# Attention and expert block on one core: the last queries' product and rotation moved among the scores, and transposed scores begun behind 38 scores

## The reference

```
h = layernorm(x)
q, k, v = h @ Wq.T, h @ Wk.T, h @ Wv.T
q, k = rotate(q), rotate(k)                    # q*cos + rotate_half(q)*sin
kf, qf = elu(k) + 1, elu(q) + 1                # linear attention
mem_out = (qf @ (kf.T @ v)) / (qf @ kf.sum)
attn = softmax(q @ k.T / 4) @ v                # per head, over 1024 keys
x = x + (sigmoid(gate)*mem_out + (1-sigmoid(gate))*attn) @ Wo.T
h = layernorm(x); top 2 of 8 experts per token, softmax of their logits
x = x + sum of weighted silu(h @ gate.T) * (h @ up.T) @ down.T
```

## Time and profile before

| | us |
|---|---|
| three runs | 425.9, 426.46, 426.72 |
| median | 426.46 |
| profiled execution | 425.57 |
| its span | 423.4 |

### The profile page before, as it was taken

The page is one execution under the profiler, slowest core; times in us unless marked ns, Lnnn a source line. Parts: engine busy times, 40 slices in busy tenths (PEclk is TensorE's granted clock), DMA queues, the critical chain, the costliest instruction groups (busy, mean ns, idle before and its releaser), DMA issues.

```text
span 423.4 us, 6988 instructions
## 1 busy us (share of the span) xinstructions
PE 398.1 (94%) x2410; PEld 228.3 (54%) x2411; DVE 253.0 (60%) x509; ACT 207.2 (49%) x395; POOL 126.3 (30%) x124
## 2 busy tenths in 40 slices
PE   8998989989999999999999799999999999999982
PEld 3463652223222322432422123699989998997981
DVE  6889889878888797679889601287224232231310
ACT  4429927676676777657566598621112212121110
POOL 6327883040301103011035240204722122312312
PEclk9999999999999999999999999999999999999997
DMA  7236914557350806203013169621544122321342
GB/s 236 106 105 100 302 36 87 95 139 244 90 185 9 263 0 211 72 8 127 2 49 138 50 210 379 181 75 39 167 106 64 25 39 31 46 39 26 37 113 25
DMA packets 22876, 45.05 MB, mean 106 GB/s; under 512 B 4448, under 2 KB 15584, under 8 KB 22016
## 3 DMA queue, kind: packets, MB, share of 16 engines
q0 software_dynamic: 9216, 30.28, 25.3%
q1 hardware_dynamic: 13152, 14.00, 12.9%
q10 hardware_dynamic: 480, 0.39, 0.3%
HBM read 23.76 MB, written 15.59 MB: 93 GB/s over the span
## 4 chain that ended last, share of the span: by engine, by line
PE 65%; DVE 11%; DMA 6%; SPq 5%; ACT 4%; issue 3%; POOL 3%; ACTq 1%; DVEq 0%; POOLq 0%
PE psum L1378 62%; DVE mem L1082 5%; DMA mem<-mem 3%; SPq L471 2%; POOL xg_d L705 2%; DMA mem<-x 2%; SPq L468 1%; DMA mem<-xg_d 1%; ACT mem L898 1%; SPq L498 1%; PE psum L1519 1%; PE psum L1651 1%; DVE mem L1025 1%; DMA xg_d<-mem 1%; ACT mem L811 1%
## 5 line engine op out<-in xcount | busy, mean ns | idle before, releaser
L1378 PE MATMUL psum<-mem 128*32 128x512 f32 (+15 forms) x2278 | 387.1, 401 | 14.7 <-DVE mem L1082 3.9
L1378 PEld LDWEIGHTS psum<-mem 128*128 128x128 f32 (+8 forms) x2278 | 215.0, 144 | 174.3 <-issue 67.1
L1082 DVE TENSOR_REDUCE mem<-psum 128x1 f32<-128x1024 f32 x128 | 152.2, 1217 | 30.4 <-PE psum L1378 28.6
L898 ACT ACTIVATE mem<-psum 128x512 f32<-128x512 f32 x256 | 137.5, 605 | 62.1 <-PE psum L1378 59.2
L916 ACT ACTIVATE mem<-psum 128x384 f32<-128x384 f32 (+3 forms) x32 | 15.1, 471 | 74.8 <-PE psum L1378 68.6
L729 POOL DMA_INDIRECT sum_d<-mem x17 | 26.7, 1570 | 69.8 <-ACT mem L924 41.2
L687 POOL DMA_DIRECT2D mem<-gate_up x21 | 15.2, 729 | 106.9 <-DMA mem<-mem 106.9
L1247 DVE COPY mem<-mem 128x3 f32<-128x3 f32 x18 | 3.0, 167 | 58.9 <-PE psum L1651 54.8
L1260 DVE TENSOR_TENSOR mem<-mem,psum 128x384 f32<-128x384 f32 (+3 forms) x32 | 16.8, 526 | 28.7 <-ACT mem L919 26.7
L924 ACT ACTIVATE mem<-psum,mem 128x256 f32<-128x256 f32 x18 | 8.5, 473 | 39.6 <-PE psum L1378 39.6
L705 POOL DMA_INDIRECT xg_d<-mem x16 | 15.8, 984 | 7.2 <-issue 4.5
(11 more groups left out here) (129 smaller groups left out, 189.3 us busy)
## 6 DMA issues: line engine op xcount, KB each, us to landing
xg_d<-mem POOLq DMA_DIRECT2D x8, 1036.0 KB, 9.5
mem<-gate_up POOLq DMA_DIRECT2D x8, 688.0 KB, 4.4
mem<-gate_up POOLq DMA_DIRECT2D x8, 624.0 KB, 6.6
mem<-down POOLq DMA_DIRECT2D x4, 1024.0 KB, 9.3
mem<-mem SPq DMA_DIRECT2D x54, 64.0 KB, 2.7
mem<-mem SPq DMA_DIRECT2D x18, 128.0 KB, 4.5
mem<-xg_d SPq DMA_DIRECT2D x16, 129.5 KB, 2.4
mem<-x SPq DMA_DIRECT2D x4, 256.0 KB, 4.7
```

Source lines behind the costliest of these rows:

```text
L898: nc.scalar.activation(prob[:, t % 8], psum[:, score_bank(n, t)], ACT.Exp, scale=HD ** -0.5).then_inc(exp_ready, 1)
L1082: V.tensor_reduce(mx[:, par, k:k + 1], banks(2 * (k % 2), 2), AX.X, ALU.max).then_inc(max_ready, 1)
L1378: return nc.tensor.matmul(*a, **k)
```

## The change

The last queries' product leaves the projections. Its four matmuls stand behind scores 1, 3, 5 and 7, in the banks that v had (4 and 5) after two of v's copies. ScalarE copies the raw product to SBUF (`q_raw`), and GpSimd does the whole rotation (`last_queries`: two products of 1024 columns, a difference and a sum of 512). VectorE no longer touches that piece. Scores are issued twice only from 8 to 15, where the transposes now stand (9, 11, 13, 15). The state is made in single products behind each of the scores 16 to 31. Masking the state stands behind the first unit's maxima instead of in front of reduction 14. Linear products 0 and 1 stand behind score 35, 2 and 3 behind 37, 4 and 5 in the loop at steps 1 and 3.

The loop begins behind FIRST = 38 scores; its steps 0 to 5 carry two scores each, until the lead of 44 is reached. ScalarE issues two of the four transfers of unit 0's maxima, and GpSimd the two transfers of first queries' second parts that ScalarE issued. SyncE sends the maxima of unit 1 ahead of `stacks(3)`. GpSimd's fills 0 to 2 no longer stand in the lead but behind `load_gate_up(0)`; the others follow one place later (`FILLS`). The last queries' middle part is made by ScalarE at step 7, and copies 2 to 5 of linear products behind exponentials 0 to 3.

```
-        QK_BANK = [4, 6, 0, 2]
+        QK_BANK = [4, 6, 0, 4]
+        TURN_BANK, STATE_BANK = [6, 7, 4, 5], 6
-        TURN_STEP, STATE_STEP, LIN_STEP = [13, 14, 15, 16], [19, 21, 23, 25], [30, 32, 35, 37, 39, 41]
+        LAST_QUERY, TURN_STEP, STATE_STEP = [1, 3, 5, 7], [9, 11, 13, 15], list(range(16, 32))
+        LIN_STEP, LIN_LATE = [35, 35, 37, 37], {1: 4, 3: 5}
...
             stacks(1)
-            max_rows(0, 0)
+            max_rows(0, 0, range(2))
             sp.wait_ge(lo_ready[1], 3)
             stacks(2)
+            max_rows(1, 1)
+            sp.wait_ge(lo_ready[2], 1)
             stacks(3)
-            sp.wait_ge(lo_ready[2], 1)
-            max_rows(1, 1)
...
+            def last_queries():
+
+                pool.wait_ge(rope_0, 3)
+                pool.wait_ge(q_copied, 2)
+                for k in range(2):
+                    nc.gpsimd.tensor_tensor(tmp[:, 2 * k:2 * k + 2], q_raw,
+                                            rope[:, k, cols(1)].unsqueeze(1).to_broadcast([P, HB, HALF]),
+                                            ALU.mult).then_inc(rope_3, 1)
+                pool.wait_ge(rope_3, 2)
+                nc.gpsimd.tensor_tensor(qT[:, 0, cols(1)], tmp[:, 0], tmp[:, 3], ALU.subtract).then_inc(rope_0, 1)
+                nc.gpsimd.tensor_tensor(qT[:, 1, cols(1)], tmp[:, 1], tmp[:, 2], ALU.add).then_inc(rope_1, 1)
...
             pool.wait_ge(mid_ready[0], 1)
             other(0)
+            pool.wait_ge(mid_ready[0], 2)
+            for g in range(GROUPS):
+                if QPART[g] == 1:
+                    to, part = second_part_rows(1, g)
+                    pool.dma_start(to, part).then_inc(q0_in, 16)
             pool.wait_ge(lo_ready[0], 3)
-            for i in range(1, 4):
+            for i in range(1, 3):
                 other(i)
...
-            FILLS = [(3, 4), (5,), (6,), (7,)]
+            FILLS = [(0, 1, 2), (3, 4), (5, 6), (7,)]
+            pool.wait_ge(xg_set, 1)
...
+            act.wait_ge(qk_ps, 4)
+            for b in range(HB):
+                nc.scalar.copy(q_raw[:, b], psum[:, QK_BANK[3] + b]).then_inc(q_copied, 1)
+            for i in range(2):
+                turned_features(i)
...
+            other_mid(0)
+            act.wait_ge(mT_ready, 1)
+            for b in range(2, 4):
+                act.dma_start(max_row(0, b), mT[32 * b:32 * b + 32]).then_inc(mrow_in, 16)
+            for i in range(1, 3):
+                other_mid(i)
+            for j in range(2):
+                lin_copy(j)
...
+                if isinstance(n, int) and n < 4:
+                    lin_copy(n + 2)
+                if isinstance(n, int) and n == 7:
+                    act.wait_ge(res_ready[2], 1)
+                    mid_part(3, slice(0, HB), resid_3).then_inc(mid_ready[2], 1)
...
-            turns(2, 1).then_inc(rope_mul, 1)
-            first_turn(3)
-            rotated(3, 0).then_inc(rope_0, 1)
-            turns(3, 1).then_inc(rope_mul, 1)
+            turn(2, 1, 1).then_inc(rope_mul, 1)
...
-                if s == 27:
+                if s == STEPS - 1:
                     mask_state()
...
-            for s in range(LEAD):
-                if s in (0, 2):
-                    pe.wait_ge(rope_mul, 3 + s // 2)
-
-                score(0, s, again=s not in TURN_STEP + STATE_STEP + LIN_STEP)
-
+            pe.wait_ge(q0_in, 16 * QPART.count(1))
+            pe.wait_ge(rope_mul, 3)
+            for s in range(FIRST):
+
+                score(0, s, again=s in range(8, 16))
+
+                if s in LAST_QUERY:
+                    k = LAST_QUERY.index(s)
+                    if k == 0:
+                        pe.wait_ge(v_ready, 2)
+                    ins = key_query(3, k // HB, k % HB)
+                    if k == len(LAST_QUERY) - 1:
+                        ins.then_inc(qk_ps, 1)
...
-                if not (isinstance(n, int) and n + LEAD >= ALL):
+                if isinstance(n, int) and n < LEAD - FIRST:
+                    for k in range(2):
+                        score(i, FIRST + 2 * t + k)
+                elif not (isinstance(n, int) and n + LEAD >= ALL):
                     score(i, t + LEAD)
+                if isinstance(n, int) and n in LIN_LATE:
+                    lin_out(LIN_LATE[n])
```

More of the change, by code:

```diff
@@ L436, in place, with queries_in, max_row, second_part_rows @@
             return 2 * i + t // STEPS, t % STEPS, 2 * STEPS * i + t
+        def queries_in(n):
+            return 16 * (GROUPS * n - QPART.count(1))
+        def max_row(sl, b):
+            return qst[SROWS:SROWS + 2, sl].rearrange("p j (k b q) -> p (j k) b q", b=4, q=32)[:, :, b]
+        def second_part_rows(i, g):
+            w, hf = QK_IDX[i]
+            to = slice(g * HD, (g + 1) * HD)
+            return (qst[to, 0] if w else kst[to, 0, :, cols(hf)]), parts[0:4 * HD, w, 1, 0, cols(hf)]
         def gate_up_pieces(to, src):
@@ L628, in _, with rest @@
+            def rest(i):
+                w, hf = QK_IDX[i]
+                pool.wait_ge(hi_ready[1], i + 1)
+                nc.gpsimd.tensor_tensor(resid_1[:, i], (kT, qT)[w][:, 1, cols(hf)], parts[:, w, 0, 1, cols(hf)],
+                                        ALU.subtract).then_inc(res_ready[1], 1)
             pool.wait_ge(mid_ready[0], 1)
             other(0)
+            pool.wait_ge(mid_ready[0], 2)
[3 more added lines that the diff above has]
+                    pool.dma_start(to, part).then_inc(q0_in, 16)
@@ L630, in _ @@
             pool.wait_ge(lo_ready[0], 3)
-            for i in range(1, 4):
+            for i in range(1, 3):
                 other(i)
             for hf in range(2):
-                feature(kfeat, kT, exp_k, hf, hf + 1)
-            pool.wait_ge(xg_set, 1)
-            pool.wait_ge(k0_in, 2 * 16 * GROUPS)
-            pool.wait_ge(q_in, 16 * GROUPS)
-            for e in range(3):
-                fill(e * T, (e + 1) * T)
-            for i in range(3):
-                w, hf = QK_IDX[i]
-                pool.wait_ge(hi_ready[1], i + 1)
-                nc.gpsimd.tensor_tensor(RESID_1[i], (kT, qT)[w][:, 1, cols(hf)], parts[:, w, 0, 1, cols(hf)],
-                                        ALU.subtract).then_inc(res_ready[1], 1)
@@ L645, in _ @@
-            for hf in range(2):
-                feature(qfeat, qT, exp_q, hf, hf + 3)
+                feature(kfeat, exp_k[:, hf], hf, hf + 1)
+            last_queries()
+            feature(qfeat, exp_q[:, :, cols(0)], 0, 3)
+            rest(0)
+            feature(qfeat, exp_q[:, :, cols(1)], 1, 4)
+            for i in range(1, 3):
+                rest(i)
             for i in range(3):
@@ L649, in _ @@
                 pool.wait_ge(mid_ready[1], i + 1)
[L650 removed]
+                nc.gpsimd.tensor_tensor(parts[:, w, 2, 1, cols(hf)], resid_1[:, i], parts[:, w, 1, 1, cols(hf)],
                                         ALU.subtract).then_inc(lo_ready[1], 1)
@@ L876, in _ @@
                                psum[:, LIN_BANK[j], 0:m * LW].rearrange("p (g c) -> p g c", g=m)).then_inc(lin_ready, 1)
+            first_hi(0)
+            first_mid(0)
+            second_keys(0)
+            act.wait_ge(rope_1, 1)
+            negated(exp_k[:, 0], kT, 0)
+            first_hi(1)
+            first_mid(1)
+            positive(kfeat, kT, 0)
+            first_hi(2)
+            grown(exp_k[:, 0], 1)
+            first_mid(2)
+            second_keys(2)
+            for j in range(4):
+                v_copy(j)
+            act.wait_ge(rope_1, 3)
+            negated(exp_k[:, 1], kT, 1)
+            positive(kfeat, kT, 1)
+            grown(exp_k[:, 1], 2)
+            act.wait_ge(qk_ps, 4)
[3 more added lines that the diff above has]
+                turned_features(i)
+            negated(exp_q[:, :, cols(0)], qT, 0)
+            positive(qfeat, qT, 0)
+            grown(exp_q[:, :, cols(0)], 3)
+            for i in range(2, 4):
+                turned_features(i)
+            for i in range(3):
+                hi_part(i, 1).then_inc(hi_ready[1], 1)
+            act.wait_ge(rope_0, 4)
+            act.wait_ge(rope_1, 4)
+            negated(exp_q[:, :, cols(1)], qT, 1)
+            positive(qfeat, qT, 1)
+            grown(exp_q[:, :, cols(1)], 4)
+            hi_part(3, slice(0, HB)).then_inc(hi_ready[2], 1)
+            other_mid(0)
+            act.wait_ge(mT_ready, 1)
+            for b in range(2, 4):
+                act.dma_start(max_row(0, b), mT[32 * b:32 * b + 32]).then_inc(mrow_in, 16)
+            for i in range(1, 3):
+                other_mid(i)
+            for j in range(2):
+                lin_copy(j)
             def turned_copy(hf, n):
@@ L1022, in turn @@
                 m, p = (tmp, tmp_odd)[i % 2], QK_BANK[i]
-                if i >= 2 and not k:
-                    dve.wait_ge((rope_0, rope_1)[b], i - 1)
+                if i == 2 and not k:
+                    dve.wait_ge((rope_0, rope_1)[b], 1)
                 return V.tensor_tensor(m[:, 2 * b + k], psum[:, p + (1 - b if k else b)],
```

120 lines of the change are left out of this document (54 added, 66 removed).

## The result

| | before | changed |
|---|---|---|
| median of 4 runs, us | 426.43 | 432.37 |
| lowest to highest, us | 425.9 to 426.72 | 432.0 to 434.04 |
| profiled execution, us | 425.57 | 432.17 |
| its span, us | 423.4 | 430.2 |
| TensorE's mean granted clock | 0.995 | 0.979 |

Changed over before is 1.0148, 95% interval 1.0116 to 1.0179: the changed kernel is **slower**, by 6 us, and outside the range of the prediction.

What follows compares the result with a forecast made beforehand. Bounds: unit 0's maxima, unit 1's start and SyncE's queue. 1.6 + 1.4 + 0.86 - 0.3 - 2.2 = 1.4 us gained: 424.2 us profiled, 425.1 us forecast median (chance 0.43); range 422.2 to 428.2 us.

Steps and rivals of the forecast that it cites:

- Start of the lead: From the projections to the first reduction: it starts at 32.6 us instead of 34.19 us, 1.6 us gained.
- The lead to the maxima: First to sixteenth reduction of unit 0: 20.4 us instead of 21.8 us, 1.4 us gained; maxima ready at about 54.4 us.
- The four steps behind a sixteenth reduction stay: Between unit 0's sixteenth reduction and its ready maxima: length unchanged, before the change from 56.04 to 57.48 us.
- GpSimd and ScalarE: Beside the lead: last query feature near 52 us, low parts near 58.5 us, second quad's stack about 1.8 us earlier.
- First transposed scores: After unit 0's maxima: no gain, and 0.3 us lost to ScalarE's middle part between two exponentials.
- Gate of unit 1: At step 32: unit 1's maxima land at 81.9 us, needed at 84.9 us; the 0.9 us wait goes, 0.86 us gained.
- What is late next: The fourth quad at step 52: last queries land at 103.3 us, TensorE waits 2.2 us; bounds nothing to 5.1 us.
- 2.1 us a key transfer: Time assumed for each 128 KB key transfer of the fourth quad beside weights and fills, between 1.8 and 3.6 us.
- rival 3: Clock falls to 1.2 GHz in the lead or behind the pause at step 52; 428.5 us or more; chance 0.06.
- Rival 2: Key stack crawls beside the fills, so score 96 waits at a price of 5.1 us; 428.0 us; chance 0.17.
- Behind step 52 the kernels have the same work: After step 52: same work and order except the fills, and a TensorE pause there is not recovered; no size given.
- The mask's wait in the lead: At scores 32 to 38 TensorE waits for the mask, idle about 45% of the time; no term in the sum.

Runs made afterwards that it cites:

- e6: e5 with GpSimd's three low parts of the second halves held until the first maxima are transposed; 424.03 us, ratio 0.9963 to the kernel before.
- e7: The changed kernel with 20 matmuls of ones ahead of its waits for queries at steps 52 and 116; 435.75 us, ratio 1.0196 to the kernel before.
- e1: The changed kernel with SyncE again sending the fourth quad's stack ahead of unit 1's maxima; 430.19 us, ratio 1.0068 to the kernel before.
- e3: The changed kernel with the fourth quad's keys issued ahead of unit 1's maxima, its queries behind them; 425.65 us, ratio 0.9984 to the kernel before.
- e5: e3 with score 35 issued eleven times; 423.85 us, ratio 0.996 to the kernel before; repeated on another chip 425.03 us, ratio 0.9986.
- e2: The changed kernel with fills 0 to 2 back in the lead, only fills 3 and 4 behind the first expert weights; 427.28 us, ratio 1.0016 to before.
- e8: The kernel before with only SyncE's order changed, unit 1's maxima ahead of the fourth quad's stack; 428.23 us, ratio 1.0042 to the kernel before.
- e9: The changed kernel with expert 0's weights and fills 0 to 2 held until the fourth quad's first queries landed; 439.04 us, ratio 1.0311 to before.
- e4: The changed kernel with fills 0 to 2 held until the fourth quad's queries landed, weights as before; 433.09 us, ratio 1.0122 to the kernel before.

## Why the prediction was wrong, point by point

The term that failed is the last of the sum, 2.2 us for the fourth quad. The wait was 4.9 us, and the half clock behind it, to which the forecast gave nothing, cost 2.2 us more in the same interval. The points in the prediction's order:

- **Start of the lead**: right, a little better. First reduction at 32.13 us for 32.6, 2.1 us gained for 1.6. VectorE's low part was through at 27.92 us (28.85 expected), and TensorE began its scores at 31.50 us after standing 1.77 us, which fits a landing in the way, as predicted.
- **The lead to the maxima**: the length was right, 20.4 us from first to sixteenth reduction, with waits of 0.50 and 0.66 us among the first eight pairs, more than the 0.3 us that the prediction named as a sign of being wrong. These were among the 1.7 us of its sum. "The four steps behind a sixteenth reduction stay" was wrong: 2.40 us instead of 1.44, with GpSimd's last f32 subtraction and first low part beside them (e6). Maxima at 54.9 us for 54.4.
- **GpSimd and ScalarE**: the last query feature was done at 51.3 us for 52. The low parts were not through at 58.5 us but at 60.0 us, and the second quad's stack began 0.3 us earlier (60.01 us), not 1.8. GpSimd waited 3.1 us for middle parts that ScalarE made only behind its two transfers of maxima, a wait that the prediction left out (line below). SyncE stood idle from 72.1 to 78.5 us behind that stack, so it cost nothing that shows.
- **First transposed scores**: right. From the first maxima to the second 23.6 us for 23.4, 0.2 us lost for 0.3.
- **Gate of unit 1**: right. No wait at step 32; the third maxima stand 3.4 us earlier for 3.6 by my terms.
- **What is late next**: the right place and the right wait, with the wrong size. By steps: keys issued from 81.24 us (80.5), landed at 94.03 (94.5), queries issued to 98.0 (98.5), need at 101.5 (101.1). All this held. The last landing did not: 106.0 us for 103.3. I had taken the contending traffic to be through at 102 us; the DMA engines were full to 104 us, and the last query transfer took 8.7 us. The wait was 4.9 us, at the end of my bounds (5.1), not 2.2. The lean to the lower end was argued from the keys, and was right for them; for the queries the nearer row was the 8.4 us that a query transfer had taken beside the same fills, which I used only for the price of a key.
- **2.1 us a key transfer** fits (12.8 us for six). The Trainium skill, page "DMA: Bandwidth & Descriptors", section "Queues, rings and completion order", has each DMA engine take turns between its queues by the packet. The 12.8 us agree with what the prediction drew from that (2.1 us, not 3.6); the turns themselves no run here shows. SyncE's queue had 30.8% from 81 to 94 us, against 7.3% in the earlier trace rows, so that the share did not carry over; the rows were longer and the competitor was weights instead of fills, and which of the two made it is open.
- **Rivals as exclusive cases**: this is the larger error. With the wait alone mis-sized the profiled execution would stand at 426.9 us; it stands at 432.2. The clock (rival 3, chance 0.06) was not a rival to the wait but followed from it: 2.2 us, and run e7 shows that the pause brings it. Rival 2 (chance 0.17) had the wait, 5.1 us, nearly right, and its 428.0 us lacked the clock. Rival 3's 428.5 us did not follow from its own numbers, since 5 us on 425.1 us are 430 us. The rest is 0.36 us more in the same interval, in e1, e3 and e5 too and not explained, 2.0 us in the interval with the half clock at 244 us, and 0.7 us in small pieces. So of the 8.0 us that the profiled execution missed by, 4.9 us are explained.
- "**Behind step 52 the kernels have the same work**": true, but not the same clock. That the falls at 217 and 244 us come from the change is not shown: they come at like places in a version without a wait (keys in front, 238 to 241 us) and in the kernel before with SyncE's order alone changed (214 to 218 and 242 to 245 us), and are missing in others. The one at 217 us cost nothing that the maxima show: that interval is 30.3 us before and changed. The Trainium skill, page "TensorE: Matmul & The Clock Gate", section "HAM oscillation — how this bites in real kernels", tells of waits for a transfer between bursts that halve the clock. The pause of 4.9 us at step 52 agrees. The mask's wait of 2.2 us in the lead, which is for VectorE, has a fall behind it in five profiles and none in two, and no run here shows what makes the difference.
- **The mask's wait in the lead** was foreseen as an idle stretch but given no term; it is 2.2 us, hides behind VectorE (0.2 us in the interval, see above), and costs only where the clock falls (1.3 us in the version with keys in front).

GpSimd's last two low parts in the changed kernel, and its wait for ScalarE:

```profile
57.71 2.27 POOL L686 TENSOR_TENSOR mem<-mem 128x512 bf16<-128x512 f32 x2 [3.09 <-ACT mem L852]
```

What stays open: what decides at a pause of 1.3 to 2.2 us whether the clock falls; the falls in the projections (11 to 15 us) and near 217 and 244 us; and the 0.36 us.

## What to carry to other kernels

A gate on one queue is a trade: count, for each block on the queue, when its own last landing is needed, and what that moved block's landing releases on other queues to run beside the rest. Here the two halves of a block had different needs: keys could go early into idle time and only the queries had to wait. And a pause of TensorE is priced with what the clock does behind it, in the same case and not as a case of its own: here some 2 us on a wait of 5.

## What the runs showed of the hardware

- A pause of TensorE of 2.9 to 7.2 us for a transfer was in all five profiles followed by half clock (1.2 GHz), which began within the pause and lasted some 7 us with pauses of up to 6.1 us and some 10 us with 7.2 us; with 4.3 us of matmuls in its place and 1.4 us of pause the clock stayed full.
- Shorter pauses did either: full clock behind 1.9 us (e2) and 1.76 us (the kernel before, 238 us), half clock behind 1.6 us (e8) and 1.80 us (changed, 243 us).
- VectorE's instructions of 16 columns took 1.0 and 1.1 us beside GpSimd's subtractions of 512 f32 columns and 0.18 us with GpSimd idle.
- A stack of six 128 KB key transfers took 8.4 us alone (e9) and 12.7 us beside 1.4 MB of weights (e4, fills held back); six of 64 KB landed 7.3 to 8.8 us after issue beside the fills, and 2.4 to 2.6 us alone (e9).
